# The product of probabilities and context in a latent attention, as three f16 products in place of f32 passes

## What is computed

```python
kv_rope = kv_c * cos[None] + _rotate_half(kv_c) * sin[None]
q_r = jnp.einsum('bshq,hqr->bhsr', q_big, W_qr)
k_r = jnp.einsum('bld,hdr->bhlr', kv_rope, W_kr)
scores = jnp.einsum('bhsr,bhlr->bhsl', q_r, k_r)
attn = jax.nn.softmax(scores, axis=-1)
ctx_c = jnp.einsum('bhsl,bld->bhsd', attn, kv_rope)    # this product
ctx_lat = jnp.einsum('bhsd,hkd->bshk', ctx_c, w_kc_kv)
out = ctx_lat.reshape(b, s, H * K) @ Wo.T
```

## Time and profile before

| what | value |
|---|---|
| median of 3 runs | 802.65 us (800.88 to 806.58) |
| profiled execution | 804.21 us |
| its span | 802.5 us |
| PE busy | 662.0 us (82%), 6210 matmuls |
| DVE busy | 423.6 us (53%) |
| ACT busy | 305.2 us (38%) |
| POOL busy | 292.9 us (37%) |
| PE's granted clock over the span | 0.879 |

### The profile page before, as it was taken

The page is one execution under the profiler, slowest core; times in us unless marked ns, Lnnn a source line. Parts: engine busy times, 40 slices in busy tenths (PEclk is TensorE's granted clock), DMA queues, the critical chain, the costliest instruction groups (busy, mean ns, idle before and its releaser), DMA issues.

```text
span 802.5 us, 17908 instructions
## 1 busy us (share of the span) xinstructions
PE 662.0 (82%) x6210; PEld 538.0 (67%) x6210; DVE 423.6 (53%) x1098; ACT 305.2 (38%) x811; POOL 292.9 (37%) x279
## 2 busy tenths in 40 slices
PE   6997677787999999999999999999885178988840
PEld 5886455675787787786786786886764067777730
DVE  1136454355467577576576576567563324434425
ACT  1122454133633634535435535445222035445310
POOL 3103386320121431531521531400403337878760
PEclk9555655979999999999999999999999579999985
DMA  8945997599200110100100100100101069999978
GB/s 225 295 98 134 206 211 151 149 343 360 69 1 3 50 36 0 61 24 0 66 20 0 66 20 0 66 2 2 64 2 50 28 167 288 306 298 305 304 111 261
DMA packets 105192, 97.12 MB, mean 121 GB/s; under 512 B 32526, under 2 KB 99088, under 8 KB 105152
## 3 DMA queue, kind: packets, MB, share of 16 engines
q1 hardware_dynamic: 73168, 62.97, 28.5%
q0 software_dynamic: 12288, 17.95, 10.3%
q10 hardware_dynamic: 19696, 15.66, 6.3%
HBM read 62.32 MB, written 35.19 MB: 122 GB/s over the span
## 4 chain that ended last, share of the span: by engine, by line
PE 52%; issue 12%; DVE 12%; DMA 8%; POOL 5%; ACT 5%; SPq 3%; POOLq 1%; ACTq 0%; DVEq 0%; PEldq 0%
PE bank L1135 6%; PE bank L1137 6%; PE bank L1136 6%; DMA expert_sums<-Wh,etok 5%; PE bank L1201 4%; PE bank L1154 4%; PE bank L1169 4%; POOL expert_sums L530 4%; PE bank L1190 4%; PE bank L1238 3%; PE bank L1183 2%; PE bank L1124 2%; PE bank L1112 2%; PE bank L1182 1%; DMA space<-L_attn_wo_scales_dram 1%
## 5 line engine op out<-in xcount | busy, mean ns | idle before, releaser
L530 POOL DMA_INDIRECT expert_sums<-Wh,etok x64 | 98.9, 1545 | 36.8 <-issue 20.4
L606 ACT ACTIVATE pr<-bank,nmax 128x257 f32<-128x257 f32 x128 | 61.2, 478 | 87.3 <-DVE nmax L830 85.8
L473 POOL DMA_INDIRECT expert_rows<-h,slot x64 | 62.6, 978 | 84.8 <-DVE slot L921 64.2
L1135 PE MATMUL bank<-space,Wh 128*128 128x128 f16 x512 | 89.4, 221 | 2.5 <-DVE space L867 1.5
L1137 PE MATMUL bank<-space,Wl 128*128 128x128 f16 x512 | 89.3, 220 | 0.0
L1136 PE MATMUL bank<-space,Wh 128*128 128x128 f16 x512 | 89.3, 220 | 0.0
L1201 PE MATMUL bank<-Cr,pT 128*128 128x64 f32 x512 | 78.8, 281 | 6.4 <-DVE On L840 5.3
L456 POOL TENSOR_TENSOR Cr<-C,Ct 128x192 f32<-128x192 f32 x64 | 39.3, 638 | 115.2 <-PE bank L1201 112.9
L1201 PEld LDWEIGHTS bank<-Cr,pT 128*128 128x128 f32 x512 | 74.8, 210 | 8.3 <-DVE On L840 5.2
L830 DVE TENSOR_REDUCE nmax<-bank 128x1 f32<-128x257 f32 x128 | 53.4, 419 | 49.5 <-PE bank L1183 44.7
L614 ACT COPY pT<-bank 128x256 f32<-128x256 f32 x128 | 47.4, 371 | 72.2 <-PE bank L1190 62.3
(11 more groups left out here) (173 smaller groups left out, 1420.8 us busy)
## 6 DMA issues: line engine op xcount, KB each, us to landing
ring<-L_ffn_gate_up_proj_dram SPq DMA_DIRECT2D x64, 192.0 KB, 4.1
expert_rows<-h ACTq DMA_DIRECT2D x8, 1284.0 KB, 12.8
Wh<-expert_rows SPq DMA_DIRECT2D x64, 160.5 KB, 4.3
ring<-L_ffn_down_proj_dram SPq DMA_DIRECT2D x64, 96.0 KB, 4.5
expert_sums<-h ACTq DMA_DIRECT2D x4, 1152.0 KB, 12.8
Wl<-expert_sums SPq DMA_DIRECT2D x16, 256.0 KB, 5.6
C<-ctx_dram SPq DMA_DIRECT2D x24, 128.0 KB, 3.8
space<-L_xattn_Wo_dram SPq DMA_DIRECT2D x8, 256.0 KB, 4.8
```

The source lines that it names most:

```text
L473: e.indirect_dma_start(XE[:, :], bass.IndirectOffsetOnAxis(ap=slot[:, k:k + 1], axis=0), h3[:, :], None, bounds_check=E * CAP - 1, oob_is_ ...
L530: e.indirect_dma_start(Y[n % NY][:, :], bass.IndirectOffsetOnAxis(ap=etok[:, n % 4:n % 4 + 1], axis=0), ye[:, n % 4], None, bounds_check=Y ...
L606: e.activation(pr[:, s, :], bank[r % 2][:, 0:NL], ACT.Exp, bias=nmax[:, s:s + 1], accum_out=rsum[:, s:s + 1]).then_inc(expd, 1)
L1135: e.matmul(dst, ah, bh, start=first and n == 0, stop=False)
```

## The change

`sum_row` now takes both operands as f16 in a high and a low part. ACT's `copy_row` writes the high part of the transposed probabilities, `pTh`, in place of `pT`. A new DVE function `pt_low` subtracts it from bank 2 and writes the low part `pTl`; it, and no longer ACT, tells `pt_ready`. POOL makes the context's parts: `Crs` holds for each sequence the high and the low part side by side. For each half of the keys `sum_row` multiplies `pTh` with both parts (128 columns) and `pTl` with the high part (64 columns). Bank 3 has 128 columns a row, the sums of high and low, and `normalise` adds both to `On` with one more linked instruction. Each sequence has one more `roped` count. `sum_row` also waits for `c_split` at the first row of a sequence.

```diff
@@ buffers
-        pT = sb("pT", [P, 2, 2, P])
+        pTh = sb("pTh", [P, 2, 2, P], f16)
+        pTl = sb("pTl", [P, 2, 2, P], f16)
+        Crs = sb("Crs", [P, BT, 2, 2, DC], f16)
@@ POOL, rope_sums
+                e.tensor_tensor(Crs[:, b, :, 0], C[:, b, 0:2], Ct[:, b, 0:2], ALU.add).then_inc(roped, 1)
                 for d in range(2):
                     e.tensor_tensor(Cr[:, b, :, d, :], C[:, b], Ct[:, b], ALU.add).then_inc(roped, 1)
+                e.wait_ge(roped, i * (3 * BT) + 3 * b + 2)
+                e.tensor_tensor(Crs[:, b, :, 1], Cr[:, b, 0:2, 0, :], Crs[:, b, :, 0], ALU.subtract).then_inc(c_split, 1)
@@ ACT, copy_row
-                e.copy(pT[:, r % 2], bank[2][:, 0:2 * P].rearrange("p (c t) -> p c t", c=2)).then_inc(pt_ready, 1)
+                e.copy(pTh[:, r % 2], bank[2][:, 0:2 * P].rearrange("p (c t) -> p c t", c=2)).then_inc(pt_high, 1)
@@ DVE
+            def pt_low(i, r):
+                e.wait_ge(pt_high, i * ROWS + r + 1)
+                if r >= 2:
+                    e.wait_ge(summed, i * ROWS + r - 1)
+                e.tensor_tensor(pTl[:, r % 2], bank[2][:, 0:2 * P].rearrange("p (c t) -> p c t", c=2), pTh[:, r % 2],
+                                ALU.subtract).then_inc(pt_ready, 1)
@@ DVE, normalise
-                link(e.tensor_tensor(On[:, b % 2], bank[3][:, 0:RB * DC].rearrange("p (r d) -> p r d", r=RB),
-                                     On[:, b % 2], ALU.add), "x", i)
+                sums = bank[3][:, :].rearrange("p (r n d) -> p r n d", r=RB, n=2)
+                for n in range(2):
+                    link(e.tensor_tensor(On[:, b % 2], sums[:, :, n], On[:, b % 2], ALU.add), "x", i)
@@ DVE, tile
                         if r < ROWS:
                             max_row(i, r)
+                        if 2 <= r <= ROWS + 1:
+                            pt_low(i, r - 2)
                         if r % RB == 2 and r > RB:
                             normalise(i, r // RB - 1)
@@ PE, sum_row
                     e.wait_ge(on_ready, i * BT + b)
-                o = DC * (r % RB)
+                    e.wait_ge(c_split, i * BT + b + 1)
+                o = 2 * DC * (r % RB)
                 for c in range(2):
-                    ins = e.matmul(bank[3][:, o:o + DC], pT[:, r % 2, c, :], Cr[:, b, c, 0, :], start=c == 0, stop=c == 1)
+                    e.matmul(bank[3][:, o:o + 2 * DC], pTh[:, r % 2, c, :], Crs[:, b, c].rearrange("p n d -> p (n d)"), start=c == 0, stop=False)
+                    ins = e.matmul(bank[3][:, o:o + DC], pTl[:, r % 2, c, :], Crs[:, b, c, 0, :], start=False, stop=c == 1)
```

More of the change, by code:

```diff
@@ L58 @@
 NLINKS = 6 + 2 * NEWTON
-XLINKS = 2 * BT
+XLINKS = 3 * BT
 SLINKS = NLINKS + 4
@@ L236, in build @@
         x_high = sem("x_high")
+        c_split, pt_high = sem("c_split"), sem("pt_high")
         x_link, r_link, n_link, sT_ready, h1_ready, rope_link, roped, scored, maxed, expd, transposed, pt_ready, summed, last_ready, on_ready = (
@@ L363, in _ @@
                 load_part(u)
-            e.wait_ge(roped, 2 * BT)
+            e.wait_ge(roped, 3 * BT)
             load_context(1)
@@ L381, in _ @@
             with e.Fori(2, T) as i:
-                e.wait_ge(roped, i * (2 * BT))
+                e.wait_ge(roped, i * (3 * BT))
                 load_context(i)
@@ L454, in rope_sums @@
                     e.wait_ge(last_ready, i * BT + (b + 1 - BT))
+                e.tensor_tensor(Crs[:, b, :, 0], C[:, b, 0:2], Ct[:, b, 0:2], ALU.add).then_inc(roped, 1)
                 for d in range(2):
                     e.tensor_tensor(Cr[:, b, :, d, :], C[:, b], Ct[:, b], ALU.add).then_inc(roped, 1)
+                e.wait_ge(roped, i * (3 * BT) + 3 * b + 2)
+                e.tensor_tensor(Crs[:, b, :, 1], Cr[:, b, 0:2, 0, :], Crs[:, b, :, 0], ALU.subtract).then_inc(c_split, 1)
             def last_rows(i, b):
                 e.wait_ge(expd, i * ROWS + RB * (b + 1))
-                e.wait_ge(roped, i * (2 * BT) + 2 * b + 2)
+                e.wait_ge(roped, i * (3 * BT) + 3 * b + 3)
                 wait_pos(e, xf, xpos(f"cT{(b - 2) % BT}", i if b >= 2 else i - 1))
```

## The result

| | before | after |
|---|---|---|
| median, us | 803.35 (4 runs, 800.88 to 806.58) | 846.68 (4 runs, 839.16 to 848.69) |
| ratio, 95% interval | | 1.0528 [1.0474, 1.0583] |
| profiled execution: time, span, us | 804.21, 802.5 | 848.34, 846.3 |

The changed kernel is 5.3% slower; 830 was forecast (range 800 to 847). The view of windows, cut at each tile's first score product as in the earlier trace rows, tiles 0, 1, 3 and 4, and in the last row the 5.4 us from the transposes for KT0 to the end of tile 4's output products. Columns as in the earlier trace rows.

The account below looks back on a forecast made before the run. PE was taken to set the pace from tile 2 on (58.54 us a tile). Waits of 7.90 us less 3.68 saved add 4.2 a tile; 21 + 2.9 + 2 + 1 = +27 gave 830 us, range 800 to 847.

Parts of the forecast that it names:

- A: Row 4: `pt_low(2)` goes before the X update on DVE, so q0 starts 0.54 us late; PE wait 1.00 us.
- B: Rows 6 to 7: two `pt_low` and the second addition delay the q2 drain by 0.99 us; PE wait 1.47 us.
- C: Row 10: `pt_low(8)` and the addition make the sums 0.63 us late on DVE; PE wait 1.09 us.
- D: Row 12: ACT's copy of row 9 and V drain come 0.63 us late, holding v1; PE wait 0.46 us.
- E: Rows 11 to 15: late ACT copies and `pt_low` make the sum of row 12 2.21 us late; PE wait 2.04 us.
- G: Row 18: `pt_low(15)` stands behind the low parts of qa and pv1, delaying row 15's sum; PE wait 1.20 us.
- F: Rows 16 and 17: h1T's copy late by 0.17 us, `pt_low(14)` behind the slot arithmetic 0.47; together 0.64 us.
- R1: Rival: DVE's idle 18.5 us a tile swallow the additions; tiles 1 to 7 keep 3.7 us each, 777 us; chance 0.10.
- R2: Rival: only waits existing today (A, C, D) grow, B and E to G are absorbed; 795 us; chance 0.12.
- the term of tile 0: Tile 0: held by the weights until DVE's last product, only G stays; +1 us, bounds -1 and +3.
- R3: Rival: PE idles 8 us more a tile and its clock falls in each, 1.7 us apiece; 840 us; chance 0.16.

Follow-up runs that it names:

- the control: The changed kernel itself run once more, unaltered, as the measure for the runs beside it: 840.59 us, ratio 1.0476 to the kernel before.
- the run in which DVE's instruction alone cost the time: Changed kernel with `pt_low` replaced by a same-size DVE instruction on constants, still waiting for ACT's cast, its result unused: 845.09 us, ratio 1.0614.
- the two-term form: Changed kernel without `pt_low` and its two products, four 64-column products into one 64-column sum a row, one addition: 791.37 us, ratio 0.9855.
- The run with the products in front: Changed kernel with tile 0's dequantising part products ahead of `pt_low` on DVE: 835.77 us, ratio 1.0381; tile 0 70.30 us in place of 73.80.
- the joined version: Changed kernel with one addition, row 4, tile-end and tile 0 reorderings on DVE, and POOL's rope products held: 811.48 us, ratio 1.0120.
- the filler: 24 small matmuls of constants on PE before KT0's transposes, result unread; added to the two-term form: 786.82 us, ratio 0.9833.
- the three-term kernel with the filler: Changed kernel with 24 small matmuls of constants on PE in the idle 1.65 us before KT0's transposes: 839.16 us, ratio 1.0531.

## Why the prediction was right, and where it was not

The direction and the mechanism held; 830 was 17 us too low, and 846.7 lies only 0.3 us inside the range of 800 to 847. Of the 17 us tile 0 is 7, falls of the clock 7, the overlap with POOL 4, the rest 2, and the steady tile itself, which I had 0.64 too long, takes 3 off again. By its steps, net of PE's saving, for a steady tile with the clock up, from the row lengths of the two kernels (row 3 and the stretch behind row 15's score product, 2.42 and 19.31 us, from the control):

| rows | places | forecast | measured |
|---|---|---|---|
| 3, 4 | A | +0.54 | -0.20 + 0.77 = +0.57 |
| 5 to 7 | B | +0.78 | -0.23 - 0.19 + 0.58 = +0.16 |
| 8 to 11 | C | +0.17 | -0.22 - 0.22 - 0.18 + 0.89 = +0.27 |
| 12 | D | +0.23 | +0.07 |
| 13 to the tile's end | E, F, G | +2.50 | +0.15 - 0.22 + 2.58 = +2.51 |
| sum | | +4.22 | +3.58 |

Right: the saving of 0.23 us a row, the 0.42 us of `pt_low`, and places A (1.00 us forecast, 1.08 measured), E and G (1.20, 1.08). At E the sum of row 12 was to start 2.21 - 0.63 = 1.58 us later behind the start of row 13 than before, and starts 1.65 later (7.10 us for 5.45). F was smaller: 0.64 forecast, a wait of 0.21. POOL's new work released PE nowhere, as priced. Both rivals with less loss fell: R1 (DVE's idle time swallows the additions) and R2 (only today's waits grow) were refuted by the waits at B, E and G, and by the run in which DVE's instruction alone cost the time.

Wrong, the step at B: 1.47 us forecast, 0.60 measured, and that is 0.62 of the 0.64 us in the sum. I moved the q2 drain by 0.35 + 0.19 + 0.45 = 0.99 us. From the start of row 5 it stands at 7.03 us before (358.90 - 351.87) and at 7.39 now (384.31 - 376.92), so it moved by 0.36. The reason is in the rows that I had read the step from. DVE's timeline, before:

```profile
350.50 1.08 DVE L930 TENSOR_TENSOR X<-X,obias 128x256 f32 x1
...
352.52 0.69 DVE L867 SCALAR_TENSOR_TENSOR space<-bank,bqk 128x512 f32<-128x512 f32 x1
...
356.35 0.78 DVE L840 TENSOR_TENSOR On<-On,rinv 128x256 f32<-128x256 f32 x1
```

and in the changed kernel:

```profile
375.54 0.42 DVE L944 TENSOR_TENSOR X<-X,obias 128x256 f32 x1
...
377.19 0.69 DVE L881 SCALAR_TENSOR_TENSOR space<-bank,bqk 128x512 f32<-128x512 f32 x1 [0.31 <-PE bank L1153]
...
382.00 0.54 DVE L854 TENSOR_TENSOR On<-On,rinv 128x256 f32<-128x256 f32 x1
```

The tile that I read had both instructions stretched beside POOL products: the update of X took 1.08 us (0.42 in the tile from 400.84, where DVE then waited 0.32 and 0.46 us for PE ahead of the q0 and q1 drains, and no row of PE was shorter), and the product with `rinv` 0.78. So DVE had slack there that this tile hid. Now it waits 0.31 us for PE, `pt_low(3)` vanishes in that slack (the q1 drain stands 2.70 us behind the start of row 5 before and 2.69 now), and the `rinv` product gives back 0.24. The other runs fit: without `pt_low` a wait of 0.21 us is left at B, with it and one addition 0.20, with neither (the two-term form) none.

Wrong, the term of tile 0: +1 forecast with a bound of +3, +7.9 measured in both profiles. I kept it held by the weights. The run with the products in front shows that DVE's order makes 3.5 us of it, and the run without `pt_low` (64.09) that all of it goes with `pt_low`: its subtractions wait for ACT behind ACT's casts of the parts, 1.05 us in the row shown. I had looked for that stall only in rows 9 and 12 of a steady tile.

Wrong by its size in the forecast's favour, R3: I gave the fall of the clock in each tile 0.16. In the first profile it came in all five tiles, 4 x 1.69 = 6.8 us more than before; in the control the falls and a little of row 3 made 6.3 us over five bases, 4.5 more than before. The forecast should have had 4 to 7 us of it: PE idles 10 us of a tile and only 3 before.

Not thought of: POOL's products overlapping DVE ahead of row 3's subtraction, 0.79 + 1.14 + 0.93 + 0.36 + 1.00 = 4.2 us over the five tiles of the first profile and under 0.3 in the control. That such an overlap stretches a DVE instruction was to be seen in the trace of before (the 1.08 at 350.50), where it cost PE nothing. The account of tiles 2 to 6 is then 5 x 3.58 + 6.8 + 4.2 = 28.9 us, and 28.9 were measured. Tile 1 was +3.2 in the first profile and -0.2 in the control, forecast +2. Tile 7 and the rest, 4.0 for 2.9 forecast.

The span of the control's profile is 7.6 us shorter than the first one's. Its tiles 2 to 6 are 6.4 us shorter, by falls and overlap, and its tile 1 is 3.4 shorter, for a reason not looked for; its first tile starts 1.9 us later. The runs didn't settle what decides at which wait the clock falls.

## What to carry to other kernels

Before an instruction is added to an engine that has "idle time", look at what it waits for and at what is queued behind it: here 0.42 us of work in DVE's order with a wait for ACT in front cost 4.5 us a tile, by the estimate above 3.8 of them even where nobody waits for its result, while four faster matmuls brought TensorE at most 2.2. Take the saving of a faster engine from the waits it will run into, not from its rows: the two-term form saves TensorE 16 x 0.28 = 4.5 us a tile (row 5: 2.43 to 2.15) and 2.2 reached the end; of the 3.7 of three products with an extra addition it was 1.0. And price the clock: with waits of over 1 us at four more places, each steady tile of the changed kernel showed one or two falls, at 0.36 to 1.69 us each. Last, read a step's slack from more than one tile: the one read here had two VectorE instructions stretched by a neighbour.

## What the runs showed of the hardware that was not expected

- The granted clock halved for about 3.4 us at a time. In the steady tiles the waits ahead of these falls were of 0.7 us (the joined version's row 11) and 1.0 to 2.1 us elsewhere, at one or two of the long waits of a tile and not at the same in each execution. With the longest wait closed (1.56 to 0.22 us) the one profile of the two-term kernel has no fall in its steady tiles where the profile without the filler has four; the three-term kernel with the filler has seven, and other waits of 1.1 us. That the filler did it is not shown.
- A fall isn't always paid: 0.36 us in row 11, where DVE was late anyway, 1.57 to 1.69 where TensorE sets the pace.
- A VectorE product of 128x256 f32 in SBUF took 1.05 us beside a GpSimd product and 0.41 without, and one of 128x1 up to 1.21 us in place of 0.16: each ended 0.01 to 0.3 us behind a GpSimd instruction. In tile 0 one of 128x1024 took 3.13 us beside such a product (median 1.2).
